# A graph network on one core: the score table filled by the sync engine, eight row buffers between the attention layers, four-deep buffers in the convolution's edge stage

## The reference

```python
# convolution (weights of an edge from 8 scalars, messages from the source node's row)
h = silu(edge_scalars @ fc_w1 / sqrt(8)) * 1.679
w = h @ fc_w2 / sqrt(64)                       # 256 weights per edge: w_a w_b w_c w_d
xg0, xg1 = y0[edge_src], y1[edge_src]
mids = concat([w_a*xg0*ea0, w_b*dot(xg1,ea1)/sqrt(3), (w_c*xg0) x ea1, (w_d*ea0) * xg1])
agg = segment_sum(mids, edge_dst, n)
out = linear layers of agg and of x
# attention layer, twice, with elu behind each
h = (x @ W).reshape(n, 4, 64)
e = leaky_relu(a_s[src] + a_d[dst], 0.2)
ex = exp(e - segment_max(e, dst)[dst])
alpha = ex / segment_sum(ex, dst)[dst]
out = segment_sum(h[src] * alpha, dst) + b
```

## Time and profile before

| | us |
|---|---|
| median of 3 runs | 5709.57 (5692.40 to 5715.53) |
| profiled execution | 5680.69, span 5678.8 |
| conv_edges | from about 200 to 2002 |
| gat_edges, layer 1 | from 2226 to about 3740 |
| gat_between | from 3744 to 4034 |
| gat_edges, layer 2 | from 4038 to about 5548 |
| gat_out | from 5550 to 5672 |

### The profile page before, as it was taken

One profiled execution on the slowest core, in us unless ns is written; L12 is line 12 of the kernel. 1 busy time (PEld: TensorE's weight loads), 2 busy tenths in 40 slices (PEclk: granted clock), 3 DMA queues, 4 the chain that ended last, 5 costly groups with the idle time before them and its releaser, 6 DMA issues. The chain is left out here.

```text
span 5678.8 us, 102477 instructions
## 1 busy us (share of the span) xinstructions
PE 4061.7 (72%) x21623; PEld 3009.8 (53%) x21624; DVE 3040.8 (54%) x7561; ACT 2499.3 (44%) x7826; POOL 3007.1 (53%) x3072
## 2 busy tenths in 40 slices
PE   2789998988998885477777777754267777777770
PEld 1577777777777773344455444532144545544450
DVE  5766666666665655345554444542245444454457
ACT  2566666766666622233333333321133333333342
POOL 2255554555555502566666666512456666666645
PEclk7899999999999997666665666665566666566665
DMA  3322222222222223344443344311334333444424
GB/s 116 105 70 70 72 72 67 73 70 70 71 70 69 71 93 100 98 117 114 115 116 105 113 116 116 98 31 44 99 104 114 111 109 114 116 114 116 115 68 138
DMA packets 253117, 533.46 MB, mean 94 GB/s; under 512 B 65502, under 2 KB 139673, under 8 KB 252916
## 3 DMA queue, kind: packets, MB, share of 16 engines
q0 software_dynamic: 136768, 380.16, 24.2%
q1 hardware_dynamic: 109128, 145.00, 8.1%
q10 hardware_dynamic: 7020, 6.40, 0.3%
HBM read 489.95 MB, written 41.38 MB: 94 GB/s over the span
## 5 line engine op out<-in xcount | busy, mean ns | idle before, releaser
L1118 POOL DMA_INDIRECT arena<-h_rows,idx x1856 | 1904.0, 1026 | 1244.6 <-issue 498.6
L1282 PE MATMUL ps<-arena,z 128*128 128x264 f32 x3712 | 1657.4, 597 | 413.4 <-DVE arena L1391 273.0
L1282 PEld LDWEIGHTS ps<-arena,z 128*128 128x128 f32 x3712 | 973.8, 288 | 739.5 <-issue 469.1
L634 POOL DMA_INDIRECT arena<-y_rows,idx x928 | 878.0, 946 | 841.9 <-DVE arena L819 573.9
L709 ACT ACTIVATE arena<-arena 128x128 f32<-128x128 f32 x3712 | 1133.0, 388 | 348.7 <-DVE arena L803 258.4
L1399 DVE TENSOR_TENSOR z<-ps,z 128x264 f32 x928 | 400.7, 432 | 1134.8 <-PE ps L1282 630.1
L765 PEld LDWEIGHTS ps<-arena 128*128 128x128 f32 x5568 | 808.4, 200 | 64.5 <-issue 8.2
L765 PE MATMUL ps<-arena 128*128 128x128 f32 x5568 | 810.4, 283 | 6.5 <-issue 6.3
L1186 ACT ACTIVATE z<-z 128x256 f32<-128x256 f32 x928 | 380.5, 410 | 949.3 <-PE ps L1282 609.8
L762 PE MATMUL ps<-arena 128*128 128x256 f32 x1856 | 630.9, 423 | 183.3 <-ACT arena L709 127.8
L1178 ACT ACTIVATE z<-iota,dst_x 128x128 f32<-128x128 f32 x1856 | 642.9, 394 | 94.9 <-ACT z L1186 4.0
(11 more groups left out here) (231 smaller groups left out, 3079.8 us busy)
## 6 DMA issues: line engine op xcount, KB each, us to landing
z<-lo_rows SPq DMA_DIRECT2D x116, 512.0 KB
arena<-h_rows,idx POOLq DMA_INDIRECT x1856
arena<-y_rows,idx POOLq DMA_INDIRECT x928
z<-seg_rows SPq DMA_DIRECT2D x232, 64.0 KB
h_rows<-arena SPq DMA_DIRECT2D x98, 132.0 KB, 1.7
arena<-h_rows SPq DMA_DIRECT2D x98, 132.0 KB, 2.1
res_rows<-z SPq DMA_DIRECT2D x98, 128.0 KB, 1.7
arena<-res_rows SPq DMA_DIRECT2D x98, 128.0 KB, 2.1
```

The source lines that it names most:

```text
L634: pool.indirect_dma_start(out=s.ring[:, r, 0:width], out_offset=None, in_=table, in_offset=bass.IndirectOffsetOnAxis(ap=s.idx[:, u, n:n + ...
L1118: pool.indirect_dma_start(out=ring[:, u * SCORED + n, :], out_offset=None, in_=h_rows, in_offset=bass.IndirectOffsetOnAxis(ap=s.idx[:, u, ...
L1282: last = t.matmul(ps[:, bank[q % 4], 0:ROW], sel[:, q % SELS, k, :], ring[:, u * SCORED + 2 * q + k, :], start=(k == 0), stop=(k == 1))
```

## The change

Three things. (1) In `conv_edges` the gather ring has 16 slots, and messages, selection matrices and weight banks have four buffers; PE, DVE and ACT take their pieces in another order; `second` multiplies over all 128 rows with a weight matrix whose other half is zero, both slots into one bank; one DVE instruction writes the 0/1 matrix of both slots. (2) In `gat_edges` SP reads the block numbers and copies the 24 columns that a pair needs from `parts_flat` into a small table in SBUF, 16 DMAs for each group, and PE's matmuls read the table at fixed addresses. (3) `gat_between` and `gat_out` have 8 row buffers (PSUM still 4), and in `gat_between` the store is body 12 of SP's list.

```diff
@@ conv_edges
-RING = 8
+RING = GROUP
-                sp.dma_start(s.w2[h * 64:(h + 1) * 64, 0:FEAT], a["fc_w2"]).then_inc(wt, 16)
+                sp.dma_start(s.w2[h * 64:(h + 1) * 64, h * FEAT:(h + 1) * FEAT], a["fc_w2"]).then_inc(wt, 16)
...
+            def second(g, u, n):
+                pair = g * IN + n
+                pe.wait_ge(h_ok, g * (IN // 2) + n // 2 + 1)
+                if not early(pair, 4):
+                    pe.wait_ge(msg_ok, pair - 3)
                 for k in range(2):
-                    rows = slice(64 * k, 64 * k + 64)
-                    last = nc.tensor.matmul(ps[:, 2 + 2 * b + k, 0:FEAT], h2[rows, q % 2, b, :], s.w2[rows, 0:FEAT], start=True, stop=True)
+                    last = nc.tensor.matmul(ps[:, 2 + n % 4, k * FEAT:(k + 1) * FEAT], h2[:, n // 2 % 2, n % 2, :], s.w2[:, k * FEAT:(k + 1) * FEAT],
+                                            start=True, stop=True)
...
+                for n in range(IN):          # PE
+                    if n % 2 == 0 and not (final and n + 4 >= IN):
+                        first(*ahead(g, u, n + 4))
+                    if not (final and n + 2 >= IN):
+                        second(*ahead(g, u, n + 2))
+                    collect(g, u, n)
...
-                for k in range(2):
-                    last = v.tensor_scalar(eq[:, b, k, :], s.iota[:, :], s.dst_x[:, bass.ds(pair * 2 + k, 1)], None, ALU.is_equal)
-                last.then_inc(eq_ok, 1)
+                if not early(pair, 4):
+                    dve.wait_ge(sel_ok, pair - 3)
+                v.tensor_tensor(eq[:, n % 4, :, :], s.iota[:, :].unsqueeze(1).broadcast_to([P, 2, P]),
+                                s.dst_x[:, bass.ds(pair * 2, 2)].unsqueeze(2).broadcast_to([P, 2, P]), ALU.is_equal).then_inc(eq_ok, 1)
...
+                for n in range(IN):          # DVE
+                    if not (final and n + 1 >= IN):
+                        messages(*ahead(g, u, n + 1))
+                    if not (final and n + 3 >= IN):
+                        select(*ahead(g, u, n + 3))
+                    if n:
+                        add(g, u, n - 1)
@@ gat_edges
+    table = part(STEPS_IN * 8 * PARTS, BF16).rearrange("p (u t n) -> p u t n", u=2, t=STEPS_IN)
             def load(g, u):
+                if isinstance(g, int) and g == 0:
+                    sp.wait_ge(parts_ok, 1)
+                if not peeled(g, 2):
+                    sp.wait_ge(look_ok, (g - 1) * STEPS_IN)
+                for t in range(STEPS_IN):
+                    block = sp.value_load(s.blk[0:1, bass.ds(g * SCORED + 2 * t, 1)], min_val=0, max_val=BLOCKS - 1)
+                    sp.dma_start(table[:, u, t, :], parts_flat[:, bass.ds(block * (8 * PARTS), 8 * PARTS)]).then_inc(table_in[u], 16)
...
-                block = pe.value_load(s.blk[0:1, bass.ds(pair * 2, 1)], min_val=0, max_val=BLOCKS - 1)
...
+                if q == 0:
+                    pe.wait_ge(table_in[u], (g - u) * (8 * STEPS_IN) + 16 * STEPS_IN)
...
-                        last = t.matmul(looked[:, :, n], hot[:, i, e:e + P], parts_flat[:, bass.ds(block * (8 * PARTS) + 8 * w, 8)],
+                        last = t.matmul(looked[:, :, n], hot[:, i, e:e + P], table[:, u, q, 8 * w:8 * w + 8],
@@ gat_between (and B = 8 in gat_out)
-    B = 4
+    B = 8
-            run_stages(sp, BLOCKS, B, [load] + [lambda k, u: None] * 5 + [store])
+            run_stages(sp, BLOCKS, B, [load] + [lambda k, u: None] * 11 + [store])
```

More of the change, by code:

```diff
@@ L729, in _, with first @@
             pe.wait_ge(wt, 16 * (GROUP + 2))
-            def first(g, u, q):
+            def first(g, u, n):
+                q = n // 2
+                k = g * (IN // 2) + q
                 if q == 0:
                     pe.wait_ge(got8[u][0], (g - u) * 8 + 16)
-                if not (isinstance(g, int) and g == 0 and q < 2):
-                    pe.wait_ge(h_ok, g * 4 + q - 1)
+                if not early(k, 2):
+                    pe.wait_ge(h_ok, k - 1)
                 for b in range(2):
-                    last = nc.tensor.matmul(ps[:, q % 2, b * P:(b + 1) * P], w8[:, 2 * q + b, :], e8[:, u, :], start=True, stop=True)
+                    last = nc.tensor.matmul(ps[:, q % 2, b * P:(b + 1) * P], w8[:, n + b, :], e8[:, u, :], start=True, stop=True)
@@ L1609, in part @@
         return v
-    quad = lambda n: part(B * n).rearrange("p (u f) -> p u f", u=B)
-    hself = quad(ROW)
-    res, t, x, neg, e, row = (quad(FEAT) for _ in range(6))
+    many = lambda n: part(B * n).rearrange("p (u f) -> p u f", u=B)
+    hself = many(ROW)
+    res, t, x, neg, e, row = (many(FEAT) for _ in range(6))
     own_act, own_dve, share, rec = own_shares(nc, s, q["own_exp"], q["shared"], part(3 * BLOCKS * HEADS))
```

223 lines of the change are left out of this document (102 added, 121 removed).

## The result

| | us, median | runs |
|---|---|---|
| before | 5,709.57 (5,685.0 to 5,727.1) | 9 |
| changed | 5,733.84 (5,720.0 to 5,760.4) | 9 |

Ratio 1.0055, 95% interval 1.003 to 1.0079: slower by half a per cent, where 5,405 us, a ratio of 0.947, were forecast. The profiled execution took 5,720.0 us, its span is 5,717.8 us (5,678.8 before), the granted clock 0.777 (0.741 before).

A forecast was written before the change was run, and what follows sets the result against it. It took circular waits around PE to bound the convolution, PE's gaps the attention edges, and one load's whole way each block between layers. Terms -135 - 3 - 120 - 37 = -295 us gave 5,405 us; 8-in-10 range 5,240 to 5,565.

The forecast's parts named there:

- Cost 0: Attention edges: SP's added 16 register reads and 16 copies, 15 us per group of 50, cost nothing.
- -165 us, four fifths taken: Attention edges: removing PE's register work ends 2.95 us idle before look-ups in 56 groups; -130 taken.
- Between the layers, -135: Stage between attention layers: overlapping loads cut a block from 5.73 to 2.8 us; -135 us (-160 to -90).
- The last stage, -3: Output stage: more buffers hardly help DVE and POOL, which take turns; -3 us (-15 to +3).
- I put this at 0 as well: Attention edges: the copies' 118,784 packets at 67 ns raise DMA share from 0.40 to 0.57, costing 0 to +30 us.
- rival A: Attention edges gain nothing, PE's gap becoming a wait for gathers or messages: 5,535 us, chance 0.17.
- most of the 0.38 us of idle PE goes: Convolution: with waits cut to 0.05 us, a pair takes 3.77 us against 3.85, -37 us over 464 pairs.
- +0.25 us for each pair: Convolution: four serial 128-row weight matmuls take 0.88 us where paired 64-row ones took 0.63.
- Layer starts, +10: Attention layer starts: copies precede line loads, look-ups begin some 20 us later; +10 us for both layers (-70 to +40).
- rival D: Attention edges: SP becomes the bound at 3.5 us per copy, 61 us per group; 6,173 us, chance 0.04.
- C: Convolution pays for serial weights and keeps its waits, because DVE stalls ("remote", 99.8 us): 5,557 us, chance 0.08.
- rival B: Attention edges: PE keeps 2.4 GHz longer, the period falls to POOL's 43.5 us per group; 5,160 us, chance 0.13.

The follow-up runs named there:

- t2: Kernel before plus eight row buffers, SyncE's table copies and TensorE's wait for them, scores still read by register: 5,635.0 us, ratio 0.9915.
- p1_again: Kernel before with only the changed stage between the layers and output stage (eight row buffers, later store): 5,507.4 us, ratio 0.9684.
- t1_no_copies: Kernel before plus eight buffers and score table, SyncE's copies left out after the first two groups: 5,553.1 us, ratio 0.9746.
- c4_rows128: Kernel before plus eight buffers, score table and the weight products in 128 zero-padded rows: 5,634.6 us, ratio 0.9882.
- p2_again: Kernel before plus eight buffers and the score table, convolution as before: 5,640.3 us, ratio 0.9876.
- a_third: The changed kernel unaltered, on a chip where the kernel before takes about 5,025 us: 4,777.8 us, ratio 0.9517.
- c5_narrow: Changed kernel, convolution's gathers behind the first group cut to 64 of 256 columns: 4,769.6 us, run once.
- c6_plain: Changed kernel, convolution's row gathers replaced by as many equally large plain SyncE transfers from fixed places: 4,774.0 us, run once.
- a_again: The changed kernel unaltered, on a chip where the kernel before takes about 5,700 us: 5,746.6 us, ratio 1.0076.
- c1_again: Changed kernel, convolution's gathers held until messages of the pair four before are done, ring still sixteen slots: 5,640.7 us, ratio 0.9915.

## Why the prediction was wrong

Two stages came out as forecast or better. What failed was the price of three terms: "Cost 0" for the copies, "-165 us, four fifths taken" for the look-ups, and -37 for the convolution. The last two took TensorE's busy time and its gaps from the records as if they were its real progress. The first priced SyncE's time and the queue's room, and not what more transfers do to engines beside which they run.

- **Between the layers, -135: right in mechanism, low in size (-173).** The step that was mis-sized took PE's 2.18 us a block from the earlier trace rows at 1.2 GHz and added waits: 2.8 us. The engine sped up to 1.16 us of matmuls, and a block takes 2.01 us, with DVE busy for 91% of it. That lies under the 2.3 us that I had called the floor.
- **The last stage, -3: right (-5).** Its blocks come 2.14 us apart where it was 2.26 ((5710.2 - 5607.4)/48, starts of L1711), and the longest of DVE's additions beside POOL still takes 941 ns.
- **"Cost 0" for SyncE's copies and "I put this at 0 as well" for their packets: wrong, and the dearest step.** Added without any use, SyncE's reads and copies cost +58 and +53 us in the layers' additions and +10 and +11 at their starts (t2 against p1_again), 132 us; by median 128. SyncE did keep up, as forecast: TensorE waits for the table at the two layer starts only. And the queue has room, 9.7% against the 8.1% of the earlier trace rows. So the share of the queue rose by 1.6 points of the whole span, not by the 17 points in the attention edges that my 67 ns for each packet gave: that was the mean of packets of 1.3 KB, and the 133,632 added ones (144 for each copy, not 128) take (0.097 x 5717.8 - 0.081 x 5678.8) x 16 / 133,632 = 0.011 us each. What the copies cost is neither SyncE's time nor the queue's. The queue's row of the page, changed kernel:

```profile
q1 hardware_dynamic: 242760, 150.76, 9.7%
```

- **"-165 us, four fifths taken" for TensorE's gap before look-ups: wrong on a chip of kind A.** t1_no_copies has the fixed addresses and no copies, and its layers take 1,403 and 1,398 us, p1's 1,396 and 1,402. That is rival A. (By the medians t1 is 0.9746 and p1 0.9684, with intervals that meet at 0.971; nothing speaks for a gain.) The gap was put down to register work because it stood before a register read; in t1, where nothing is read, it is 47.3 us of 1,000. Groups of t1_no_copies, 2500 to 3500 us:

```profile
L1289 PE MATMUL ps<-arena,z 128*128 128x264 f32 x1276 | 533.5, 563 | 227.4 <-DVE arena L1398 158.2 <-issue 43.1 <-DVE z L1406 21.5
...
L1246 PE MATMUL ps<-z 128*128 128x8 bf16 x1902 | 87.9, 173 | 47.3 <-issue 47.3
```

- **Convolution, "most of the 0.38 us of idle PE goes", -37: wrong (+119).** On a chip of kind A the idle time did not come from the circle of waits alone but from a TensorE that falls behind beside gathers. With a ring of eight GpSimd never issued more than six gathers without a pause from 300 to 1900 us, mostly two; with sixteen half of them stand in runs of eight to ten, 1.25 us apart, as here in the changed kernel (the first and the last of ten):

```profile
442.91 0.95 POOL L635 DMA_INDIRECT arena<-y_rows,idx  x1 [0.30 <-issue]
...
454.15 0.94 POOL L635 DMA_INDIRECT arena<-y_rows,idx  x1 [0.30 <-issue]
```

  The pace of the old ring, put back into the changed kernel, holds the runs to six again and gives 85 of the 110 us back (2,151, 2,066 and 2,041 in the sheet). The other 25 are about the 20 us that the new form costs on a chip of kind B as well, and no more than the spread. That the length of the runs is what costs is argued from this, not shown: TensorE is late for as long with the pace (759 us) as without (772). The step "+0.25 us for each pair" failed by itself too: c4_rows128 is 6 us under p2_again, and the runs of either spread over some 30 us. Per pair (22 matmul records) a chip of kind B takes 3.26 us before and 3.29 after, so 0.03 for the whole new form. The Trainium skill ("TensorEngine Tiling (Array Packing)", Key Properties) says that a change of the tiling mode drains TensorE, and the traces agree with a price for it: L762 behind 64-row products takes 424 ns, behind 128-row ones 396 (kind A), and 406 against 380 on kind B, where the records can be trusted. I had looked for that price in the weights' own matmuls alone.
- **Layer starts, +10: the sign right, +17.** ACT's wait for the last look-up, changed kernel on kind A and (a_third) on kind B:

```profile
2438.96 0.28 ACT L1163 ACTIVATE z<-ps 128x128 f32<-128x128 f32 x1 [90.45 <-PE ps L1251]
```

```profile
2019.76 0.28 ACT L1163 ACTIVATE z<-ps 128x128 f32<-128x128 f32 x1 [32.28 <-PE ps L1251]
```

The pace of 0.7 us per instruction in the earlier trace rows was a sign of the kind of chip, not of the kernel. I used it for the start alone and for rival D, and priced every other stage as if TensorE went by its records.

- **Rivals.** D had the right sign and the wrong engine: SyncE did not become the bound. C named the "remote" stall and priced it at the serial weights. On chips of kind B the forecast's sum nearly came out, ratio 0.9517 where 5,405/5,709.6 is 0.947, but in part by luck: -186 us for the buffers where -138 stood, -88 for the table (-120), +26 for the convolution (-37), so errors of both signs cancel. POOL is the bound of the attention edges there, as rival B had it.

**Open.** What slows TensorE on a chip of kind A is not settled: the issuing by GpSimd, the number of packets or their bytes. c5_narrow and c6_plain were made for that and fell on chips of kind B. That the packets themselves take longer there is excluded: q0, which has the gathers, is busy for 24.2% of 16 x 5731.5 us in a_again and 28.9% of 16 x 4770.2 us in a_third, for 136,768 packets each, 162 and 161 ns a packet. t2's reads and copies by SyncE add to the cost, but beside gathers, so they don't tell whether GpSimd's part is needed; and whether it is the reads or the copies was not told apart on a chip of kind A. Nor is it known what makes a chip of one kind or the other. The traces of kind A also lack records of semaphores where gathers run (in a_again 344 rises for the 387 messages from 310 to 1890 us; in a_third none lack there, but 58 of 381 do for the look-ups of the attention edges from 2200 to 3200 us), and every time here is of an execution that was recorded, so a part of the recording in the slowing is not excluded. That pauses between gathers help is shown for the convolution (c1_again) and only there.

## What to carry to other kernels

Before pricing waits, look for "remote" idle time and "issue" gaps inside an unbroken run of matmuls: they say that TensorE is behind its records, and then its busy share is no bound and a gap before a register read is no price of the read. That a queue has room does not make added transfers free; price them by what transfers already stretched where they stood beside TensorE. Time a change on more than one chip before it is kept: the score table was worth -1.8% on one and +2.0% on another.

## What the runs showed of the hardware that was not expected

- The kernel before takes 5,022 to 5,026 us on some chips and 5,692 to 5,710 on others, and without gathers the convolution runs alike on both (8,027 records in 1,200 us). With them, on the slower kind alone, TensorE raises the semaphore of the collects up to 6.9 us behind the modelled ends of its matmuls (c1_again); on the other kind it is 15 ns at most in this stage (a_third). The granted clock is not the reason: paced, it was 0.99 on a chip of kind A, and there were still only 6,745 records.
- GpSimd's gathers are not slower there: their mean is 953 ns (a_again) and 958 ns (a_third) from 300 to 1900 us.
- SyncE's own small instructions spread as well. The changed kernel on a chip of kind A (a_again), count, ns min/median/max:

```profile
L1138 SPq TENSOR_LOAD <-blk x928: 2/271/1396, 2353.5 to 5506.0; - x186
L1138 SPq SEQ_ASSERT  x928: 2/18/1589, 2354.3 to 5506.5; - x186
```

and on kind B (a_third):

```profile
L1138 SPq TENSOR_LOAD <-blk x928: 265/273/493, 1988.8 to 4529.3; - x186
L1138 SPq SEQ_ASSERT  x928: 18/18/37, 1989.6 to 4529.8; - x186
```

The medians agree, but on kind A single ones take 1.4 to 1.6 us. So the slowing is not TensorE's alone; that the same cause stops both is a guess.
